# Causal attention of layer 1: mask products that address only their 64 output partitions

## The reference, cut to what matters

```python
def _causal_attn(q, k, v):
    scores = jnp.einsum('bthd,bshd->bhts', q, k) * scale
    mask = jnp.tril(jnp.ones((t, t), dtype=bool))
    scores = jnp.where(mask, scores, -jnp.inf)
    attn = jax.nn.softmax(scores, axis=-1)
    return jnp.einsum('bhts,bshd->bthd', attn, v)
...
ctx = _causal_attn(q, k, v)
conv_out = conv(ctx) + conv_b
ctx2 = _causal_attn(conv_out as heads, k, v)
out = ctx2.reshape(b, s, d) @ out_w.T + out_b
```

## Time and profile before

| | |
|---|---|
| median of the runs | 3385.98 us |
| the profiled execution | 3388.66 us |
| its span, first to last instruction | 3386.8 us |
| TensorE busy | 3115.7 us, 92% |
| VectorE busy | 2534.1 us, 75% |
| ScalarE busy | 2057.6 us, 61% |
| mean granted TensorE clock | 0.975 of full speed |

### The profile page before, as it was taken

The page is one execution under the profiler, slowest core; times in us unless marked ns, Lnnn a source line. Parts: engine busy times, 40 slices in busy tenths (PEclk is TensorE's granted clock), DMA queues, the critical chain, the costliest instruction groups (busy, mean ns, idle before and its releaser), DMA issues. The chain is left out here.

```text
span 3386.8 us, 83147 instructions
## 1 busy us (share of the span) xinstructions
PE 3115.7 (92%) x33099; PEld 1852.8 (55%) x33099; DVE 2534.1 (75%) x5014; ACT 2057.6 (61%) x4153; POOL 877.2 (26%) x783
## 2 busy tenths in 40 slices
PE   6887799999999999999999999789999999999997
PEld 5776322222223677777777777545555554555554
DVE  5777788888887476677667766677887877778874
ACT  6775288888888443333434334247777666776776
POOL 3322311111111322342233224224342211111110
PEclk9998799999999999999999999889999999999999
DMA  4100122222221110010001101223333232222222
GB/s 142 36 20 4 54 80 83 78 81 84 81 75 53 34 30 30 23 33 29 29 23 33 35 23 30 49 77 95 90 93 81 79 98 86 80 78 80 84 61 67
DMA packets 234976, 204.91 MB, mean 61 GB/s; under 512 B 74340, under 2 KB 190852, under 8 KB 234500
## 3 DMA queue, kind: packets, MB, share of 16 engines
q1 hardware_dynamic: 228484, 195.50, 20.1%
q0 software_dynamic: 6144, 4.72, 1.0%
HBM read 73.61 MB, written 59.39 MB: 39 GB/s over the span
## 5 line engine op out<-in xcount | busy, mean ns | idle before, releaser
L1624 DVE TENSOR_REDUCE b_maxima<-psum 128x2 f32<-128x1024 f32 (+3 forms) x768 | 779.8, 1041 | 227.0 <-PE psum L1421 216.9
L1565 ACT ACTIVATE b_prob<-psum 128x512 f32<-128x512 f32 (+2 forms) x1536 | 725.5, 526 | 298.4 <-PE psum L1454 292.0
L1624 DVE TENSOR_REDUCE c_maxima<-psum 128x2 f32<-128x1024 f32 x512 | 592.5, 1213 | 58.1 <-PE psum L1415 57.3
L1565 ACT ACTIVATE c_prob<-psum 128x512 f32<-128x512 f32 x1024 | 547.2, 600 | 113.9 <-PE psum L1447 97.3
L2378 PEld LDWEIGHTS psum<-consts_layer,a_hid 128*128 128x128 f32 x4096 | 477.5, 192 | 53.8 <-issue 53.6
L2368 PE MATMUL psum<-a_x1t,consts_layer 128*128 128x512 f32 x1024 | 462.1, 595 | 20.8 <-ACT a_hid L2438 13.8
L2378 PE MATMUL psum<-consts_layer,a_hid 128*128 128x128 f32 x4096 | 479.0, 275 | 0.0
L2438 ACT ACTIVATE a_hid<-psum,consts_layer 128x512 f32<-128x512 f32 x512 | 347.0, 687 | 197.2 <-PE psum L2368 190.5
L1478 PE MATMUL psum<-b_prob,b_v 128*32 128x128 f32 (+3 forms) x5632 | 398.4, 371 | 15.9 <-ACT b_c L1572 15.4
L1447 PE MATMUL psum<-b_qa,b_ka 64*128 64x512 bf16 (+3 forms) x2048 | 344.2, 303 | 40.1 <-ACT b_prob L1565 26.0
L2605 DVE SCALAR_TENSOR_TENSOR a_acc<-psum,a_gprob,a_acc 128x128 f32<-128x128 f32 x512 | 143.7, 343 | 261.1 <-PE psum L2378 233.1
(11 more groups left out here) (407 smaller groups left out, 4200.7 us busy)
## 6 DMA issues: line engine op xcount, KB each, us to landing
b_qa<-b_part SPq DMA_DIRECT2D x192, 128.0 KB
b_context<-b_c SPq DMA_DIRECT2D x64, 256.0 KB, 2.1
c_qa<-c_part SPq DMA_DIRECT2D x96, 128.0 KB, 2.5
c_ka<-c_part SPq DMA_DIRECT2D x96, 128.0 KB, 2.6
b_ka<-b_part SPq DMA_DIRECT2D x96, 128.0 KB
c_context<-c_c SPq DMA_DIRECT2D x32, 256.0 KB, 2.1
b_scale<-b_inverse SPq DMA_DIRECT2D x64, 128.0 KB
b_unscaled<-b_context SPq DMA_DIRECT2D x64, 128.0 KB
```

Source lines behind the costliest of these rows:

```text
L1565: self.nc.scalar.activation(out, src, ACT.Exp, scale=SCALE).then_inc(self.s.free, 1)
L1624: self.nc.vector.reduce_max(out, src, X).then_inc(self.m.free, 1)
```

## The change

Each mask product takes only the 64 columns of `pick[n]` that belong to its n, and writes only the 64 output partitions of n: the weights are 64 x 64 in place of 64 x 128. Where two heads share a bank (t = 2 and 3), one product masks both: its moving operand is the triangle twice (`qmask` and `kmask` are now two copies side by side, which costs two more casts at the setup), its output two blocks of 64 columns at a distance of w. The mask products of both heads therefore stand behind both score products, where they stood behind each. The score product of the second head in a bank has `start` false. In a quad this makes 48 mask products where there were 64 (scores and maxima together). `tensor_turn`, the rings and the other engines' code stay.

```diff
-            self.qmask = sb("qmask", [P, HALF], BF16)
-            self.kmask = sb("kmask", [P, HALF], BF16)
+            self.qmask = sb("qmask", [P, 2, HALF], BF16)
+            self.kmask = sb("kmask", [P, 2, HALF], BF16)
...
-            nc.gpsimd.tensor_copy(self.qmask[:, :], self.K("qmask"))
-            nc.gpsimd.tensor_copy(self.kmask[:, :], self.K("kmask")).then_inc(self.tables_ready, 1)
+            for k in range(2):
+                nc.gpsimd.tensor_copy(self.qmask[:, k, :], self.K("qmask"))
+                last = nc.gpsimd.tensor_copy(self.kmask[:, k, :], self.K("kmask"))
+            last.then_inc(self.tables_ready, 1)
...
-                last = nc.tensor.matmul(out[:, half, k0:k0 + w], qa[rows, hh, t * P:(t + 1) * P], ka[rows, hh, 0:w], start=True, stop=not self.causal)
-            if self.causal:
-                for n in range(2):
-                    for half in range(2):
-                        rows = slice(half * HALF, (half + 1) * HALF)
-                        k1 = k0 + t * P + n * HALF
-                        last = nc.tensor.matmul(out[:, half, k1:k1 + HALF], self.pick[n][rows, :], self.qmask[rows, :], start=False, stop=n == 1)
+                last = nc.tensor.matmul(out[:, half, k0:k0 + w], qa[rows, hh, t * P:(t + 1) * P], ka[rows, hh, 0:w], start=k == 0, stop=not self.causal)
+        if self.causal:
+            heads = 1 + self.together(s)
+            for n in range(2):
+                k1 = t * P + n * HALF
+                for half in range(2):
+                    rows = slice(half * HALF, (half + 1) * HALF)
+                    own = out[n * HALF:(n + 1) * HALF, half, 0:heads * w].rearrange("p (k x) -> p k x", k=heads)[:, :, k1:k1 + HALF]
+                    last = nc.tensor.matmul(own, self.pick[n][rows, n * HALF:(n + 1) * HALF], self.qmask[rows, 0:heads, :], start=False, stop=True)
         last.then_inc(self.m.ready, 1)
...
+        if self.causal:
+            heads, k0 = 1 + self.together(s), 0 if self.together(s) else q0
+            for n in range(2):
+                for half in range(2):
+                    rows = slice(half * HALF, (half + 1) * HALF)
+                    own = outs[half][n * HALF:(n + 1) * HALF, k0:k0 + heads * w].rearrange("p (k x) -> p k x", k=heads)[:, :, n * HALF:(n + 1) * HALF]
+                    last = nc.tensor.matmul(own, self.pick[n][rows, n * HALF:(n + 1) * HALF], self.kmask[rows, 0:heads, :], start=False, stop=True)
+                    if n == 1:
+                        last.then_inc(self.s.ready, 1)
```

More of the change, by code:

```diff
@@ L1441, in tensor_scores @@
             k0 = k0 if self.together(s) else q0
-            done = not self.together(s) or k == 1
             for half in range(2):
@@ L1446, in tensor_scores @@
                     pe.wait_ge(self.s.free, self.s.room("exp", p, s, jobs[half]))
-                last = nc.tensor.matmul(outs[half][:, k0:k0 + w], ka[rows, hh, t * P:(t + 1) * P], qa[rows, hh, q0:S], start=True, stop=not self.causal)
+                last = nc.tensor.matmul(outs[half][:, k0:k0 + w], ka[rows, hh, t * P:(t + 1) * P], qa[rows, hh, q0:S], start=k == 0, stop=not self.causal)
                 if not self.causal:
                     last.then_inc(self.s.ready, 1)
[L1450 to L1456, removed]
+        if self.causal:
[7 more added lines that the diff above has]
+                        last.then_inc(self.s.ready, 1)
     def tensor_values(self, pe, p, s, half=None):
```

## The result

The changed kernel takes 3518.58 us (median of two runs, 3515.85 to 3521.31), against 3385.98 before: ratio 1.0393, 95% interval 1.0375 to 1.0412, so 4% slower. The forecast was 3514.

What follows compares the result with a forecast made beforehand. TensorE nearly bounds the second attention (1086 of 1191 us in flight); 3388.7 + 218 of TensorE work - 90 absorbed by waits = 3517, stated as 3514 since the median is 2.7 lower; 8-in-10 range 3432 to 3598.

Steps and rivals of the forecast that it cites:

- A change of cut costs 0.092 us: Second attention on TensorE: each switch between products of different array rows and columns adds 0.092 us, 64*128 to 64*64 included.
- Rival A: Mask entries: no drain between cuts sharing their 64 rows, so 47 us less on TensorE, 3350 us; chance 0.08.
- 2402 more changes: Around the second attention's mask groups: 1536 entries and 866 new exits, each a change of cut, 141 and 80 us.
- A place occupies 0.060 or 0.086 without the change: Mask groups: 1024 one-head places hold TensorE 0.060 us each, 512 two-head places 0.086, 105 us in all.
- The load of narrow weights: Masks' first weights: halving them makes the load no cheaper; uncovered load and starts add 0.033 us to each group.
- TensorE's work +218: Second attention: streaming -12, entries +141, new exits +80, products behind them +9, so +218 us; load bounds +183 to +245.
- Waits take back 90 of 105: Second attention: of TensorE's 105 us open, mostly waits on other engines and DMA, 90 absorb added work.
- hidden 40: TensorE's waits: records hide part of each behind its modelled end, so the pool may be some 40 us larger.
- B, waits cover almost all: Second attention: load at its low bound +183, all 105 and the hidden 40 absorbed, +38, 3424 us; chance 0.05.
- C, the clock gives way: Second attention: idle stretches lower the granted clock; five per cent gives 40 us more, 3555, or 3600; chance 0.07.
- D, only the upper half's products change cut: Mask products with output from partition 0 keep the wide cut; 46 us more, about 3550; chance 0.05.
- The masks' followers: ScalarE and VectorE idle behind masks grows from 292.0 and 216.9 us; masks leave 0.14 to 0.17 before next scores.

Runs made afterwards that it cites:

- masks_together: Changed kernel, only reordered: at the first unit of each slot both score products come first, then both masks; 3466.88 us, ratio 1.0228.
- all_64x64: Changed kernel with the second attention's score products also cut into halves of 64 output partitions, so scores and masks are all 64*64; 3370.01 us, ratio 0.9944.

## Why the prediction was right, point by point

- *A change of cut costs 0.092 us.* Right, also for the one pair that the kernel before does not contain. Into the masks: 0.32 against 0.22 (0.320 against 0.227 in the medians). Rival A, no drain between cuts that share their 64 rows, is refuted by every entry. The Trainium skill (TensorEngine Tiling (Array Packing), Key Properties) states that a change of mode drains the engine. The traces agree in that each of these changes has the step; what the array does in it they do not show. The prediction's "the trace agrees for each pair that it holds" goes too far: in the kernel before, projection L3068 (128*128, 512 columns in f32) leads to the transposition L1428 (128*16) in 0.429 us in 13 of 14 places, where it takes 0.525 when a product with 64 rows follows (L3072, the same size). (The fourteenth stood at half of full speed.) That step is missing, for a reason that no run tests. It is the same before and after, so the count of added changes does not depend on it.
- *2402 more changes.* 2400 were counted.
- *A place occupies 0.060 or 0.086 without the change.* Measured 0.156 and 0.183 with the exit's change in it, so 0.06 and 0.09; without any exit 0.053 and 0.080 (masks_together). Right within 0.01.
- *The load of narrow weights.* Its record is 103 ns. Of the 0.033 taken for first load and starts, masks_together shows 0.026 (0.053 less the 0.027 of streaming), so the term was a little large. By the Trainium skill (TensorE: Matmul & The Clock Gate, LDWEIGHTS) a load of 64 columns is estimated at 53 ns, which would have put the sum about 30 us higher; that much does not show.
- *TensorE's work +218.* Measured +225 (1018 to 1243), or +209 without the line ahead in the kind. Put together from the steps, it is 95 for the places (1024 x 0.053 + 512 x 0.080), 143 for the entries (1536 x 0.093) and 89 for the new exits (864 x 0.103), less 117: +210.
- *Waits take back 90 of 105.* The waits fell by 95, counted from start to start. By the records the open time fell by 59 only (105 to 46); the rest was behind the modelled ends, the "hidden 40" of the prediction. So the sum 218 - 90 = 128 came out as 225 - 95 = 130. Nearly all of the 95 went at full clock (149 to 58 us). That the sum is within 2 us owes something to luck: the 90 were to come out of the open 105, which gave 59; the estimate of how much goes was a judgement, and masks_together shows that the same judgement fails by 30 us in another place.
- *B, waits cover almost all:* no, 73 us of waits stay. *C, the clock gives way:* no. The mean is 0.975 in both stages, and what the intervals at half speed have above full-speed work is 18 us before and 15 after, so the clock added nothing. *D, only the upper half's products change cut:* no, all four are marked 64*64 and start 0.003 us apart, with no step between n = 0 and n = 1.
- *The masks' followers.* ScalarE's and VectorE's idle behind the masks was to grow from 292.0 and 216.9: it did, to 397.6 and 340.9. A mask of one head leaves 0.156 before the next scores, inside the 0.14 to 0.17 given as the sign; one of two heads leaves 0.183, above it.

## What to carry to other kernels

Before packing small products into quarters of TensorE's array, write down the cut (rows and columns of the weights, rounded up) of every product in the order in which they run, and count the places where it changes: here each cost 0.09 us, three times what the narrow mask of one head saved (0.057 to 0.028). If the neighbours can take the same cut, even with twice as many of them, the loss is gone (3370 against 3518 us) and a little is gained on the kernel before (0.6%). And read what TensorE really occupies from start to start: the busy share counted modelled ends, and hid the steps of 0.09 us and a third of the waits alike.

## What the runs showed of the hardware that was not expected

Doubling the score products of the second attention (4096 more, each with half of the output partitions) cost TensorE almost nothing: the net work of all_64x64 is 30 us lower than before, near the 33 that were expected, and behind masks of the same cut 512 columns lead to their mask in 0.220 us in both kernels. The transposition L1428 (128*16) behind a 128*128 projection shows no step, as said above. And the slope from work to time is not one number: over the kernel before, 107 us of work cost 41 us (0.38), 138 cost 81 (0.59), 225 cost 133 (0.59); from the changed kernel on, 118 more cost 109 (0.92), when waits had gone from 168 to 73 us and fell no further. As the work is uncertain by some 20 us, the first of these shares is rough; the last stands apart from the others.
